# Delta rule: sixteen units in one block on absolute turns, the preparation of a unit begun 44 turns before it

## The chip, the cores and the metric

The program runs on one core of one Trainium2 chip. The metric is the device time of one execution, in microseconds, taken as the median of the runs. The program is a small model of four layers, each with an attention part and a feed-forward part, and everything is computed in float32 (f32). The change lies in one of the eight parts, the attention of the last layer, which takes 1852.8 us of the profiled execution's span (from 2876.4 to 4729.2). A core has an engine for matmuls (PE, its weight loads shown apart as PEld), VectorE (DVE), ScalarE (ACT) and GpSimd (POOL), each with its own instruction stream, and they wait for each other by semaphores. PSUM, where matmuls write, has eight banks here, `P[0]` to `P[7]`.

## The reference, cut to what matters

The last layer's attention is a gated delta rule over 512 tokens, for 8 batches and 8 heads, with keys of 128 and values of 32:

```python
h = layernorm(x) * (1 + ca) + sa
beta = sigmoid(h @ Wb) * 2.0
g = -exp(A_log) * softplus(h @ Wa + dt_bias)
alpha = exp(g)
q = l2norm(silu(causal_conv4(h @ Wq)))      # (8, 512, 8 heads, 128)
k = l2norm(silu(causal_conv4(h @ Wk)))
v = silu(causal_conv4(h @ Wv))              # (8, 512, 8 heads, 32)
def step(state, inp):                       # a scan over the tokens
    q_t, k_t, v_t, a_t, b_t = inp
    retained = einsum('bhvk,bhk->bhv', state, k_t)
    state = a_t * (state - b_t * retained x k_t) + b_t * v_t x k_t
    return (state, einsum('bhvk,bhk->bhv', state, q_t))
out = out * rsqrt(mean(out * out) + 1e-5) * o_norm_w * silu(h @ Wg)
x = x + ga * (out @ Wo)
```

## The kernel before

**Units, chunks, turns.** The work of `delta_rule` is cut into 16 units: a batch and one half (`g`) of its heads, four heads. A unit has four chunks of 128 tokens, and within a chunk the recurrence is solved as a triangular system. A chunk takes nine turns. In each turn every engine is given, in this order: a step that solves the chunk before (table `SOLVE`: state, four solves with a "before" between them, finish), in turns 0, 3 and 6 a part of making the next chunk's matrices (`MAKE`), a step that inverts this chunk's triangular block by products of 32x32 (`INVERT`), and then pieces that prepare the unit that comes next. So a unit has 36 turns, and there is no other order than this one, written out by `in_turn` and followed by all engines alike.

**The pieces.** `norm` is the layer norm (two matmuls of 128x512, once per batch), `small` and `gate` the small vectors of beta and g, `taps` the convolved queries and keys: sixteen pieces of two matmuls of 128x512 each (L1841), every second of which is followed by a silu on ACT (`taps_done`, L1962), a square on POOL (L1918) and a matmul that sums squares (`squares`, L1849). `values`, `keys` (transposes), `norms`, `scale`, `rms` and `out` (the output projection of a batch) are the rest. The matmuls of the chain of chunks are L1778 (state), L1783 and L1790 (before, solve), L1796 and L1803 (finish), L1740 (products of the inversion), L1725 (`MAKE` part 0) and L1733 (parts 1 and 2).

**Blocks.** A `Block` is a piece of program with one stream for each engine, and between two of them is a barrier, `k.end()`, in which the semaphores are cleared. `delta_rule` has ten after its setup: `delta_first` prepares unit 0, `delta_second` runs it, seven of `delta_units` run two units each (first the second half of a batch, with the norm of the next batch among its pieces, then the first half of the next batch, with the output of the batch before), and `delta_last` runs unit 15. In a block a unit's pieces are those of the unit that follows, in turns that `pieces(u)` gives; `taps` stand from turn 1 or 6 to turn 24.

**Banks.** `P[0]` holds the inversion's products, `P[1]` what `MAKE` needs, `P[2]` and `P[7]` take turns as the bank of the solves, `P[3]` (`few`) is for small sums, and `P[4]` to `P[6]` are a ring for the large pieces. A piece of the ring waits (`emptied`) until the one three before it was read. `QK` has queries and keys of 8 heads, so of two units.

**Tables.** ACT works from a table that belongs to a function (silu from one, exp and ln from another); a change is an instruction `ACT_TABLE_LOAD`, either put there by `table` (L1997) or by the compiler before a function that needs it.

## Time and profile before

| what | us |
|---|---|
| median of 3 runs | 4829.73 |
| lowest and highest | 4824.34, 4837.81 |
| the profiled execution, its own time | 4835.91 |
| its span | 4833.6 |
| `delta_first`, from 2876.4 | 64.7 |
| `delta_second`, to 3051.1 | 110.0 |
| the seven `delta_units`, to 4620.6 | 1569.5 |
| `delta_last`, to 4729.2 | 108.6 |

The blocks begin at 2876.4, 2941.0, 3051.1, 3276.0, 3501.2, 3726.8, 3948.2, 4170.7, 4394.8 and 4620.6. A row of the view by stretch gives, for each engine, the busy us in a stretch with the number of instructions, and PEclk, the granted clock of PE as a share of its full speed: 1.00 is 2.4 GHz, 0.50 is 1.2 GHz, and what lies between is a mean of the two over the stretch. In a timeline a row has the start, the length and the instructions, and in brackets the idle time of the engine just before with what ended it. The span in 40 slices shows the stage from slice 24 to 39.

### The profile page before, as it was taken

What the parts mean: (1) busy time and instruction counts of PE and PEld (TensorE: products, weight loads), DVE (VectorE), ACT (ScalarE), POOL (GpSimd) and SP (SyncE); (2) the same over time, 40 slices, a digit from 0 to 9 for tenths busy, and PEclk for the clock granted to TensorE, in tenths of its full rate; (3) what the DMA queues carried; (4) which work ended last, traced back from release to release, by engine and by line L of the source; (5) the groups of instructions that cost most, each with busy time, mean ns of one, the idle gap of its engine ahead of it and who ended that gap; (6) DMA issues with size and microseconds to landing.
All of it is one profiled execution on the core that took longest, in us unless ns stands there. A gap on an engine that the chain in (4) does not pass through costs nothing. (4 is left out here: it accounts for less than half of the span.)

```text
span 4833.6 us, 125108 instructions
## 1 busy us (share of the span) xinstructions
PE 3978.2 (82%) x55640; PEld 2527.1 (52%) x55640; DVE 2423.2 (50%) x6070; ACT 1502.6 (31%) x2781; POOL 746.2 (15%) x740
## 2 busy tenths in 40 slices
PE   3657776999857888888887958999998999999985
PEld 1225664344335565655564324666666666666671
DVE  3556775232277777777771122444343443434344
ACT  2443333455432222222222322323232332323223
POOL 1112221000012212121110002211121212212111
PEclk8777666999855656555556979888898989999966
DMA  2000000322000000000000010000000000000000
GB/s 74 0 0 1 1 1 6 65 35 35 15 1 3 3 3 3 3 3 3 3 3 15 0 54 1 2 2 2 2 2 2 2 2 2 2 2 2 2 2 19
DMA packets 18968, 45.93 MB, mean 10 GB/s; under 512 B 4864, under 2 KB 8320, under 8 KB 17408
## 3 DMA queue, kind: packets, MB, share of 16 engines
q1 hardware_dynamic: 18432, 37.95, 3.2%
q8 instruction: 439, 7.19, 0.6%
q14 instruction: 97, 0.79, 0.1%
HBM read 35.71 MB, written 2.23 MB: 8 GB/s over the span
## 5 line engine op out<-in xcount | busy, mean ns | idle before, releaser
L1841 PE MATMUL ps<-d_hp,d_w_qk 128*128 128x512 f32 x1024 | 519.5, 632 | 8.0 <-ACT d_QK L1962 8.0
L1841 PEld LDWEIGHTS ps<-d_hp,d_w_qk 128*128 128x128 f32 x1024 | 179.0, 193 | 226.1 <-issue 200.8
L1031 PE MATMUL ps<-g_Q,g_K 32*32 32x32 f32 (+1 forms) x12288 | 273.1, 248 | 22.8 <-issue 8.3
L1031 PEld LDWEIGHTS ps<-g_Q,g_K 32*32 32x32 f32 x12288 | 237.9, 135 | 66.7 <-PE ps L1031 38.9
L852 PE MATMUL ps<-ex_hs,w_c_fc 128*128 128x512 f32 x512 | 232.9, 598 | 19.7 <-DVE ex_hs L818 19.7
L1063 PE MATMUL ps<-g_S,g_V 32*64 32x32 f32 x4096 | 160.8, 287 | 86.2 <-DVE g_H L1239 65.0
L1938 ACT ACTIVATE d_F<-ps 128x128 f32<-128x128 f32 x256 | 70.9, 277 | 514.8 <-PE ps L1740 514.3
L863 PE MATMUL ps<-ex_r,w_c_proj 128*128 128x512 f32 x512 | 230.0, 592 | 0.0
L826 DVE TENSOR_TENSOR ex_r<-ex_r 128x512 f32<-128x512 f32 x128 | 88.5, 693 | 277.5 <-ACT ex_r L840 277.5
L840 ACT ACTIVATE ex_r<-ps 128x512 f32<-128x512 f32 x256 | 151.6, 593 | 236.1 <-PE ps L852 236.1
L2070 DVE COPY d_W<-ps 32x128 f32<-32x128 f32 x256 | 73.0, 285 | 278.7 <-PE ps L1790 276.4
L1898 POOL TENSOR_TENSOR d_M<-d_A,w_joins 128x128 f32<-128x128 f32 (+1 forms) x128 | 112.1, 897 | 580.7 <-ACT d_A L1932 580.7
L1063 PEld LDWEIGHTS ps<-g_S,g_V 32*64 32x64 f32 x4096 | 127.7, 203 | 135.3 <-DVE g_H L1239 75.8
L1918 POOL TENSOR_TENSOR d_sq<-d_QK 128x512 f32<-128x512 f32 x128 | 133.3, 1044 | 401.4 <-ACT d_QK L1962 347.9
L2067 DVE TENSOR_TENSOR d_r<-d_r,ps 32x128 f32<-32x128 f32 x192 | 55.0, 286 | 260.6 <-PE ps L1783 244.1
L1047 PE MATMUL ps<-g_V,g_KT 32*32 32x64 f32 x4096 | 156.9, 292 | 21.7 <-issue 1.2
L852 PEld LDWEIGHTS ps<-ex_hs,w_c_fc 128*128 128x128 f32 x512 | 98.3, 192 | 143.8 <-issue 122.9
L1928 ACT ACTIVATE d_D<-d_D 128x512 f32<-128x512 f32 x64 | 40.3, 629 | 412.6 <-DVE d_D L2013 412.6
L863 PEld LDWEIGHTS ps<-ex_r,w_c_proj 128*128 128x128 f32 x512 | 97.3, 190 | 122.5 <-issue 106.7
L1740 PE MATMUL ps<-d_X,d_M 32*32 32x32 f32 x8192 | 128.9, 198 | 38.8 <-DVE d_X L2036 24.3
L1893 POOL TENSOR_TENSOR d_D<-d_D,w_upto 128x512 f32<-128x512 f32 x64 | 85.4, 1335 | 469.7 <-ACT d_D L1928 469.7
L1733 PE MATMUL ps<-d_QK 128*128 128x128 f32 x1024 | 157.2, 300 | 0.8 <-DVE d_P L2018 0.8
(462 smaller groups left out, 8313.4 us busy)
## 6 DMA issues: line engine op xcount, KB each, us to landing
ex_root<-gate_rows SPq DMA_DIRECT2D x8, 2048.0 KB, 15.3
...
```

The lines of the kernel that those rows point to most:

```text
L826: e.tensor_tensor(r[:, n % 2, f], r[:, n % 2, f], r[:, n % 2, f], ALU.mult).then_inc(dve.steps, dve.did(f"r{n}{f}"))
L840: e.activation(r[:, n % 2, f], hidden(f), ACT.Relu).then_inc(act.steps, act.did(f"r{n}{f}"))
L852: e.matmul(hidden(f), k.w["c_fc"][:, n % E, ts(f, C)], hs[:, n % 3], start=True, stop=True).then_inc(pe.steps, pe.did(f"u{n}{f}"))
L863: e.matmul(total(b), k.w["c_proj"][:, x, f, :], r[:, n % 2, f], start=(x == 0 and f == 0), stop=(x == E - 1 and f == F - 1)).then_inc(pe.s ...
L1031: ins = e.matmul(later(scored, n_), keys_, queries(n_, planes, r, 4 * i + j), start=(turn_ == 0 and part == 0 and n_ != 1), stop=(part == ...
L1047: ins = e.matmul(P[2 * odd + 1][ts(h4, 32), 256 + j * 64:320 + j * 64], KT[rows, (KR, KI)[part], i, ts(h4, 32)], V[rows, i, 4 * sg + h4, ( ...
L1063: ins = e.matmul(P[4 + bank][ts(second, 64), t], V[rows, i, 4 * sg + h4, (slice(32, 96), slice(0, 64))[part]], S[rows, i % 2, h4, part, :] ...
L1733: ins = e.matmul(mk[:, ts(h, C)], QK[:, 1, H, t], QK[:, part - 1, H, t], start=True, stop=True)
L1740: ins = e.matmul(inv[rows, h], stationary[rows, h], moving[rows, h], start=True, stop=True, tile_position=(32 * j, 32 * j))
L1841: ins = e.matmul(b, w_qk[:, j, c, ts(H, C)], hp[:, j:j + T], start=(j == 0), stop=(j == TAPS - 1))
L1898: e.tensor_tensor(M[:, a, levels], A32[:, a].unsqueeze(1).to_broadcast([C, many, 4, 32]), k.w["joins"][:, levels].unsqueeze(2).to_broadcas ...
L1918: e.tensor_tensor(squares(x), qk, qk, ALU.mult).then_inc(pool.steps, pool.did(f"{tag}sq{x}"))
```

## The change

All sixteen units stand in one block, and the ten blocks, with the nine barriers between them, are one. A turn has an absolute number, 36 to a unit, and `pieces_at` gives each piece of unit `u` a turn counted from the unit's own start: `norm` 55 turns before (even units), `small` and `gate` from -36 to -27, the sixteen `taps` at -44, -42 and so on to -14, their silu and squares behind them, `values` from -15, `keys` from -10 and `norms` from -9. Within a unit, turns 0 to 22 then hold twelve pieces of `taps` of the next unit and turns 28 to 34 four of the one after, one in every second turn, and turns 23 to 27 hold none. `QK` has 12 heads, three units; `hp`, the normed input with its modulation, has two copies; the norm works in `OT`. One bank, `P[2]`, is for the solves, and the state step now also waits for `out` of the chunk before. The ring has four banks, `P[4]` to `P[7]`, and takes in the norm's first matmul, `small` and the sums of the gates. The norm reads `X`, and the modulation `k.mod`, directly: POOL's copy of a batch (L1905) and DVE's of `modb` (L2098) and `m_out` are gone. The product with `o_norm_w` on POOL stands in a turn of its own (`weigh`). The plain query and key weights are no longer loaded with the layer's other weights, but by a DMA into `QK` in the block `delta_start`, which ends when they are there. A `table` piece stands in every ninth turn. In the delta rule the new program has 195 table loads where there were 127; the matmuls are the same in number and kind.

```diff
-        xb = k.sb("d_xb", [C, T], stack=s)
-        hp = k.sb("d_hp", [C, T + 3], stack=s)
-        QK = k.sb("d_QK", [C, 2, NH, T], stack=s)
+        hp2 = k.sb("d_hp", [C, 2, T + 3], stack=s)
+        hp_of = lambda u: hp2[:, u // 2 % 2]
+        QK = k.sb("d_QK", [C, 2, 12, T], stack=s)
...
+            @block.sync
+            def _(e):
+                e.dma_start(w_plain, k.dram["Wqk3"]).then_inc(dma.steps, dma.did("plain"))
+                e.wait_ge(dma.steps, dma.at("plain"))
...
-        bank = lambda i: P[(2, 7)[i % 2]]
+        bank = lambda i: P[2]
...
+            for turn in range(0, NU * TU, NI):
+                put(0, turn - 1, "table", 0)
+            for u in range(NU):
+                if u % 2 == 0:
+                    for turn, x in ((-55, 1), (-53, 2), (-51, 3)):
+                        put(u, turn, "norm", x)
+                for turn, piece in ((-36, ("small", 0)), (-35, ("gate", 0)), (-33, ("gate", 1)), (-30, ("gate", 2)), (-27, ("gate", 3)), (-27, ("gate", 4))):
+                    put(u, turn, *piece)
...
-                    t = begin + (last - begin) * x // 15
-                    at[t] += [("taps", x)]
-                    if x % 2:
-                        at[12 if 9 <= t + 1 < 12 else t + 1] += [("taps_done", x // 2)]
-                        at[max(t + 3, sums + 2 + x // 2)] += [("squares", x // 2)]
+                    put(u, 2 * x - 44, "taps", x)
+                for x in range(8):
+                    put(u, 4 * x - 41 + (x == 6), "taps_done", x)
+                    put(u, 4 * x - 38, "squares", x)
+                for turn, x in zip((-15, -14, -13, -12), range(NT)):
+                    put(u, turn, "values", x)
+                for turn, x in zip((-13, -12, -11, -11), range(NT)):
+                    put(u, turn, "values_done", x)
+                put(u, -9, "weigh", 0)
+                for x in range(NT - 1):
+                    put(u, 3 * x - 10, "keys", x)
+                    put(u, 3 * x - 9, "keys_done", x)
                 for x in range(5):
...
-                at[3].insert(1, ("table", 0))
-            if u["next"]:
-                for t in (8, 17, 26):
-                    at[t] += [("table", 0)]
+                    put(u, x - 9, "norms", x)
+                put(u, -3, "scale", 0)
+                for turn, x in ((9, 0), (10, 1), (11, 2)):
+                    put(u, TU + turn, "rms", x)
+                if u % 2:
+                    for turn, x in ((13, 0), (14, 1), (16, 2)):
+                        put(u, TU + turn, "out", x)
...
+                for turn in range(min(at), NU * TU + max(max(at) - NU * TU, len(SOLVE)) + 1):
+                    u, i, step = turn // TU, turn % TU // NI, turn % NI
+                    if turn >= 0 and step < len(SOLVE) and 0 < turn // NI <= NU * NT:
+                        n = turn // NI - 1
+                        solve(n // NT, n % NT, *SOLVE[step])
+                    n = turn // NI + 1
+                    if step in MAKE and 0 <= n < NU * NT:
+                        make(n // NT, n % NT, MAKE[step])
+                    if 0 <= turn < NU * TU:
+                        invert(u, i, *INVERT[step])
+                    for piece in at.get(turn, ()):
+                        prepare(*piece)
...
+                if what == "norm" and x < 3 or what in ("small", "values", "keys", "out") or what == "taps" and x % 2 == 0 or (what, x) == ("gate", 2):
+                    ring[u, what, x] = len(order)
+                    order.append((u, what, x))
 
...
+            ring_bank = lambda u, what, x: P[4 + ring[u, what, x] % 4]
...
-                            if c % 2 in outs:
-                                e.wait_ge(dve.steps, dve.at(f"out{outs[c % 2]}"))
-                            outs[c % 2] = n
+                            if u or c:
+                                e.wait_ge(dve.steps, dve.at("out" + (chunk(u, c - 1) if c else chunk(u - 1, 3))))
                             if c:
...
-                            e.matmul(few, k.w["center"][:], xb[:], start=True, stop=True).then_inc(pe.steps, pe.did("nc"))
+                            emptied(e, u, "norm", 1)
+                            e.matmul(ring_bank(u, "norm", 1), k.w["center"][:], flat(k.X[:, u // 2:u // 2 + 1, :]), start=True, stop=True).then_inc(pe.steps, pe.did(tag + "nc"))
...
-        block_of("delta_first", [unit("s", None, None, True, norm=0)])
-        block_of("delta_second", [unit("a", 0, None, True)])
-        for b in range(B - 1):
-            block_of("delta_units", [unit("a", 1, True, True, norm=b + 1), unit("b", 0, True, True, out=b)])
-        block_of("delta_last", [unit("a", 1, True, False, out=B - 1)])
+        all_units("delta_units")
```

**PE, unit 9, turns 7 to 10** (the second half of batch 4). Before, with the sums of the gates (L1858, L1859) and two matmuls of `taps` (L1841) in turn 9:

```order
L1740 MATMUL ps<-d_X,d_M 32x32 x16
L1841 MATMUL ps<-d_hp,d_w_qk 128x512 x2
L1796 MATMUL ps<-d_zz,d_P 128x32 x4
L1740 MATMUL ps<-d_Y,d_F 32x32 x16
L1841 MATMUL ps<-d_hp,d_w_qk 128x512 x2
L1725 MATMUL ps<-w_upto,d_g 128x128 x4
L1858 MATMUL ps<-d_g,w_upto 128x16
L1859 MATMUL ps<-d_g,w_ones 128x16
L1841 MATMUL ps<-d_hp,d_w_qk 128x512 x2
L1790 MATMUL ps<-d_r,d_Y 32x32 x4
```

The same turns now, where L1727 is a solve, L1684 the products, L1733 and L1737 the finish, L1669 `MAKE` part 0, L1771 `taps` and L1779 `squares`:

```order
L1727 MATMUL ps<-d_r,d_Y 32x32 x4
L1684 MATMUL ps<-d_X,d_M 32x32 x16
L1733 MATMUL ps<-d_zz,d_P 128x32 x4
L1684 MATMUL ps<-d_Y,d_F 32x32 x16
L1771 MATMUL ps<-d_hp,d_w_qk 128x512 x2
L1669 MATMUL ps<-w_upto,d_g 128x128 x4
L1727 MATMUL ps<-d_r,d_Y 32x32 x4
L1684 MATMUL ps<-d_X,d_M 32x32 x16
L1771 MATMUL ps<-d_hp,d_w_qk 128x512 x2
```

What stood between `MAKE` part 0 and the solve of turn 10 is gone, and between the `taps` of turn 8 and those of turn 10 there are `MAKE` part 0, a solve and products.

**PE, the end of unit 8 and the start of unit 9.** Before:

```order
L1796 MATMUL ps<-d_zz,d_P 128x32 x4
L1803 MATMUL ps<-d_ze,d_KT 128x32 x4
L1740 MATMUL ps<-d_Y,d_F 32x32 x16
L1710 UNCONDITIONAL_BRANCH
L1711 UNCONDITIONAL_BRANCH
L1778 MATMUL ps<-d_S,d_QK 128x32 x8
L1725 MATMUL ps<-w_upto,d_g 128x128 x4
L1830 MATMUL ps<-d_w_v,d_hp 128x128 x4
L1831 MATMUL ps<-w_Wg,d_hp 128x128
```

Now, where L1715 is the state step and L1754 `small`:

```order
L1733 MATMUL ps<-d_zz,d_P 128x32 x4
L1737 MATMUL ps<-d_ze,d_KT 128x32 x4
L1684 MATMUL ps<-d_Y,d_F 32x32 x16
L1715 MATMUL ps<-d_S,d_QK 128x32 x8
L1669 MATMUL ps<-w_upto,d_g 128x128 x4
L1754 MATMUL ps<-w_Wab,d_hp 128x16 x4
L1771 MATMUL ps<-d_hp,d_w_qk 128x512 x2
```

The two branches of the barrier are gone, the state step and `MAKE` part 0 follow the products at once, and `small` and `taps` stand where `values` stood.

**ACT, the same place.** Before, L1986 being the copy of keys, L1938 that of the products, L1928 the exp of `MAKE`, L1948 the square of the norm and L1958 the silu of values:

```order
L1986 ACTIVATE d_KT<-ps 128x512
L1710 UNCONDITIONAL_BRANCH
L1922 UNCONDITIONAL_BRANCH
L1997 ACT_TABLE_LOAD
L1928 ACTIVATE d_D<-d_D 128x512
L1938 ACTIVATE d_F<-ps 128x128
L1948 ACTIVATE d_sq<-ps 128x512
L1958 ACT_TABLE_LOAD
L1958 ACTIVATE d_values_gates<-ps 128x2x128 x3
```

Now, L1910 and L1864 being the same copies, L1886 the silu of `taps`, L1854 the exp of `MAKE`, L1889 to L1892 the functions of the gates:

```order
L1864 ACTIVATE d_F<-ps 128x128
L1879 ACT_TABLE_LOAD
L1886 ACT_TABLE_LOAD
L1886 ACTIVATE d_QK<-ps 128x512
L1854 ACT_TABLE_LOAD
L1854 ACTIVATE d_D<-d_D 128x512
L1864 ACTIVATE d_F<-ps 128x128
L1889 ACTIVATE d_beta<-d_beta 128x4x4
L1890 ACTIVATE d_t<-d_t 128x4x4
L1892 ACT_TABLE_LOAD
L1892 ACTIVATE d_beta<-d_beta 128x4x4
```

The table of the `table` piece (L1879) is at once followed by another, for the silu of `taps`, and the exp behind it needs a third.

## Rows read from the trace of the kernel before

**Rows 1.** The page, busy time by engine and the granted clock (40 slices of 121 us).

```profile
PE 3978.2 (82%) x55640; PEld 2527.1 (52%) x55640; DVE 2423.2 (50%) x6070; ACT 1502.6 (31%) x2781; POOL 746.2 (15%) x740
...
PEclk8777666999855656555556979888898989999966
```

**Rows 2.** Busy time by stretch: length, busy us of each engine, granted clock, DMA share.

```profile
2876.00:2941.00 65.00, 52.87 (x136) 22.75 (x136) 7.45 (x24) 21.84 (x38) 11.88 (x12) 0.82 0.00 0
2941.00:3051.00 110.00, 97.71 (x1520) 65.03 (x1520) 39.56 (x126) 29.47 (x70) 21.74 (x21) 0.89 0.01 2
...
3501.00:3727.00 226.00, 211.75 (x3217) 144.62 (x3218) 95.39 (x296) 64.85 (x151) 44.20 (x43) 0.89 0.01 2
3727.00:3948.00 221.00, 207.23 (x3216) 140.74 (x3216) 95.19 (x295) 64.46 (x150) 44.19 (x43) 0.92 0.01 2
...
4621.00:4729.00 108.00, 87.95 (x1560) 76.89 (x1559) 47.72 (x144) 22.46 (x49) 10.99 (x10) 0.61 0.01 2
```

**Rows 3.** The same view, two stretches inside the pair that begins at 3726.8.

```profile
3755.00:3784.00 29.00, 28.86 (x397) 15.47 (x395) 14.54 (x44) 12.78 (x28) 8.30 (x8) 1.00 0.01 2
...
3926.00:3947.00 21.00, 19.71 (x380) 16.43 (x380) 10.72 (x36) 4.60 (x15) 2.94 (x3) 0.74 0.01 2
```

**Rows 4.** The same view around two falls of the clock.

```profile
3809.00:3812.50 3.50, 3.42 (x58) 3.34 (x59) 1.15 (x6) 1.42 (x2) 1.04 (x1) 0.98 0.00 0
3812.50:3819.00 6.50, 6.50 (x41) 4.57 (x44) 2.62 (x10) 0.63 (x1) 0.35 (x1) 0.50 0.01 4
...
3863.50:3867.00 3.50, 2.01 (x50) 1.76 (x49) 2.33 (x7) 0.70 (x2) 0.54 (x1) 0.99 0.00 0
3867.00:3870.40 3.40, 3.40 (x5) 0.87 (x4) 2.21 (x7) 0.97 (x6) 1.11 (x1) 0.50 0.00 0
```

**Rows 5.** Timeline of PE in unit 8: start, length, instructions, idle before and its releaser.

```profile
3858.57 1.98 PE L1841 MATMUL ps<-d_hp,d_w_qk 128*128 128x512 f32 x4 [1.00 <-ACT d_QK L1962]
...
3863.50 1.05 PE L1725 MATMUL ps<-w_upto,d_g 128*128 128x128 f32 x8
...
3866.41 0.45 PE L1740 MATMUL ps<-d_X,d_M 32*32 32x32 f32 x32 [1.49 <-DVE d_X L2036]
3866.79 3.66 PE L1841 MATMUL ps<-d_hp,d_w_qk 128*128 128x512 f32 x4
...
3872.09 1.98 PE L1841 MATMUL ps<-d_hp,d_w_qk 128*128 128x512 f32 x4
...
3879.41 1.02 PE L1849 MATMUL ps<-d_sq,w_picks 128*8 128x512 f32 x2 [1.58 <-POOL d_sq L1918]
```

**Rows 6.** Timeline of PE in unit 9, the same turn of its unit.

```profile
3978.80 1.96 PE L1841 MATMUL ps<-d_hp,d_w_qk 128*128 128x512 f32 x4
...
3980.97 0.45 PE L1740 MATMUL ps<-d_X,d_M 32*32 32x32 f32 x32
```

**Rows 7.** Timeline at the end of the block that ends at 3948.

```profile
3946.17 0.29 DVE L2087 TENSOR_TENSOR d_S<-d_S,ps 128x128 f32<-128x128 f32 x1 [2.32 <-PE ps L1803]
...
3946.69 0.29 DVE L2090 TENSOR_TENSOR d_O<-d_o,d_qn 128x128 f32<-128x128 f32 x1
...
3948.23 1.46 PE L1778 MATMUL ps<-d_S,d_QK 128*128 128x32 f32 x6 [1.51 <-PEq L70]
```

**Rows 8.** Timeline of PE at a finish step of unit 8, turn 26.

```profile
3920.98 1.41 PE L1796 MATMUL ps<-d_zz,d_P 128*128 128x32 f32 x8 [2.27 <-DVE d_ze L2076]
```

**Rows 9.** Groups of ACT by line: busy us and mean ns, idle before them.

```profile
L1955 ACT ACT_TABLE_LOAD x56 | 71.8, 1283 | 1.0
L1962 ACT ACT_TABLE_LOAD x40 | 51.3, 1283 | 0.7
```

**Rows 10.** Timeline of ACT, a table load and the function after it.

```profile
2895.30 1.28 ACT L1962 ACT_TABLE_LOAD   x1
2896.60 0.60 ACT L1962 ACTIVATE d_QK<-ps 128x512 f32<-128x512 f32 x1
```

**Rows 11.** DMA issues, KB each, median us from issue to landing.

```profile
w_Wqk<-in_Wqk_dram SPq DMA_DIRECT2D x1, 1024.0 KB, 4.6
```

366 lines of the change are left out of this document (123 added, 243 removed).

## The prediction, as written before the changed kernel ran

> **What bounds the kernel now.** I read the page's busy line and clock line first [rows 1], then busy time by stretch [rows 2, 3], then the places where PE's clock falls [rows 4], then PE's timeline with its idle times [rows 5 to 8]. PE is the busiest engine (82% of the span, DVE 50%, ACT 31%) [rows 1]. In the delta rule this is sharper: in a block of two units PE is busy 207.2 of 221 us, DVE 95, ACT 64, POOL 44 [rows 2]. PE sets the time, so only three things can move it: matmul work, PE's waits, and its clock. The change leaves the work as it is. The clock is the large lever. A pair takes 226 us at a granted 0.89 and 221 at 0.92 [rows 2] with the same instructions; with two levels, 1.2 and 2.4 GHz, 0.92 means 2 x 0.08 x 221 = 35 us at the low one, 0.89 means 50 us (48 with the mean of 0.90 over the pairs). A stretch full of `taps` is granted 1.00 with PE busy 28.86 of 29; the last chunk, without `taps`, 0.74 [rows 3].
>
> **What a us at the low clock costs.** Four matmuls of `taps` took 3.66 us low and 1.98 high [rows 5], so a low us loses 0.46 us where PE is full. Across pairs, 0.03 of clock on 226 us is 13.4 us low for 5 us of time, 0.37. I use 0.40 to compare pairs. At full clock the pair of 221 us would take 221 - 0.40 x 35 = 207.
>
> **What makes the clock fall.** Twice: with PE busy 2.01 of 3.5 us it went to 0.50 for the next 3.4 us; and, more telling, with PE busy 3.42 of 3.50 us, but on small products, it was 0.50 for the next 6.5 us [rows 4]. Being busy is not enough here; stretches without 512-wide matmuls fall. The Trainium skill ("TensorE: Matmul & The Clock Gate", Part 1: The HAM clock gate) says that the clock follows how busy PE has been lately. Read as busy time, the 3.42 of 3.50 contradicts it, and by it a pair with its waits gone would hardly fall; that is the first rival below.
>
> **The change part by part, for a pair (two units), at full clock, from 207.**
> - *Barrier.* PE idles 1.51 us for it, and DVE and ACT start behind [rows 7]; 1.0 more for that, estimated. -2.5.
> - *Ring of four, taps evenly in every second turn.* In unit 8 `taps` waited 1.00 us for a bank that ACT had yet to read, and `squares` 1.58 us for POOL [rows 5]. With four banks and silus four turns apart both go: -2.6 in this unit. The other unit of the pair I take at half of that (bounds 0 and 2.6): -4 together.
> - *One solve bank.* The state step now waits for `out` of the chunk before, not only for S: DVE finished S at 3946.17 + 0.29 and `out` at 3946.69 + 0.29, so 0.5 us later [rows 7]. PE stands idle for it only where no `taps` lie behind the products: turn 35 of both units and turn 17 of one. Behind it in PE's stream is everything, `MAKE` part 0 too. 3 x 0.5 = +1.4; were all eight exposed, +4.
> - *Places that lose their cover.* With two `taps` matmuls between `MAKE` part 0 and the solve, products of turn 10 had no idle time in unit 9 [rows 6]; without, 1.49 us in unit 8 [rows 5]. Now unit 9 has none either: +1.5, and 0.5 for turn 27, where no `taps` stand. The finish step's 2.27 us in turn 26 [rows 8] stays, since turns 23 to 27 are as bare as before. +2.
> - Together 207 - 2.5 - 4 + 1.4 + 2 = 204.
>
> **The clock after.** `taps` were packed (two turns of three) and left chunk 3 bare; now one turn in two has them, and turns 28 to 34 too. So chunk 3, at 0.74 before, fills up, while dense chunks get thinner. I count the stretches without `taps` between two pieces of them: 9 to 10, 17 to 18 (odd units), 23 to 27, and 35 to 0 in each unit, eight or so in a pair, of which I expect four of five to drop the clock, for 3.4 to 6.5 us each as in [rows 4]: about 30 us low in a pair (bounds 8 and 60). At 0.40 to 0.46 each that is +12.5, so a pair takes 216.5 against a mean of 224.3 (1569.5 / 7). I round to 216: **-8.3 a pair, -58 in seven**.
>
> **The ends.** *First pieces of the next unit.* By starting 44 turns ahead, four pieces of `taps`, a norm, a square and small sums leave the seven pairs and go into the start. `taps` are 8 x 0.49 = 4.0 us [rows 5]; the rest I estimate at 3.7 from the same 0.49 for a wide matmul (two of the norm, two of squares, and small ones). -7.7 here. *Start.* First and second block take 64.7 + 110.0 us with PE busy 52.9 and 97.7 [rows 2]. The moved 7.7 us fall into the wait at the first block's end (some 12 us of its 65 are idle), a barrier goes (-2.5), the bare end of unit 0 fills: 174.7 to 170, -4.7. *End.* The last block runs at 0.61 [rows 2]; its chain of DVE and PE stays, a barrier goes, out waits come: -1.6.
> *Setup.* The load of the plain weights took 4.6 us to landing [rows 11], hidden among the layer's other loads; now little of DVE's setup runs beside it. +4 (bounds 0 and 5). The copies of `X` and `modb`, which go, cost nothing on PE's path, save at the very start of the stage, where PE waits for the first, which I leave in the rounding.
>
> **Table loads.** 68 more at 1283 ns [rows 9] are 87 us of ACT, 5.5 us a unit: ACT goes from 64.5 to about 75.5 of 216 us. The function after a load began 1.30 us after the load's start [rows 10], so nothing beyond the load is lost. The Trainium skill ("ScalarE: Activation LUTs", What ACT_TABLE_LOAD costs) adds a drain of 1380 ns to each; by that the 68 would be 181 us of ACT, still not the bound; these rows show no drain. On PE's path a load counts where PE waits for a function behind it: the exp of `MAKE` once a unit, which has three turns until PE needs it, and copies of products, which PE waits for. I take 0; if the exp's load came through in every unit, 16 x 1.28 = +21 us, and that is in the range.
>
> **Sum.** -58 - 7.7 - 4.7 - 1.6 + 4 = -68. The profiled execution took 4835.91 (span 4833.6), 6.2 over the median of 4829.73. So 4768 for a run like the profiled one, 4762 for the median; I say **4765 us**.
>
> **Rivals.**
> 1. *The clock hardly falls.* If a piece of `taps` in every second turn is enough to hold it, some 8 us a pair are low: 204 + 3.5 = 207.5, -16.8 x 7 = -118, with the ends -128: **4702**. For it: 29 us at 1.00 where PE was full [rows 3]. The rule of the Trainium skill named above, with PE busy some 97% of the time, leads here too. Against it: the fall after 3.42 of 3.50 busy [rows 4]. Chance 0.23.
> 2. *Little gain.* The removed waits return behind others (the ze wait behind the out wait, table loads before the copies), or 40 us stay low: a pair 220 to 223, in all **4800 to 4815**. Chance 0.12.
> 3. *No change.* The same with some 45 us low, a pair 224, and start, end and setup adding up to little: within 14.5 us of **4830**. Chance 0.11.
> 4. *Slower: thinner `taps` keep the clock down.* Place: the dense chunks 0 to 2, which today run at up to 1.00 [rows 3]. Before, the clock that had fallen was back at 1.00 after four wide matmuls in a row [rows 4, 5]; with one piece of two matmuls every second turn it may stay low through whole chunks. Price 0.46 us for each low us. From 204, it decides at (224.3 - 204) / 0.46 = 44 us low a pair; at 60 low a pair takes 204 + 27.6 = 231.6, +51 in seven pairs, less 10 at the ends: **about 4870**. Against it: chunk 3 at 0.74 with no `taps` at all [rows 3] is as thin as it can be and is only 21 us long. Chance 0.14.
> That the change does not do what it says is no rival of its own: the order of instructions shows the barriers gone and the matmuls equal.
>
> **Numbers.** Forecast, 4735 to 4800: 0.40. The five cases make 1.00. The range, **4695 to 4840**, takes in the forecast, rival 1 down to 4695, rivals 2 and 3 and the table loads' +21; outside are the slower case and the tail of rival 1. A measurement of this kernel can tell about 0.3%, 14.5 us, from no change. Faster by more: 0.40 + 0.23 + 0.12 = 0.75. Within: 0.11. Slower by more: 0.14. The likeliest case's own range is 4735 to 4800.
>
> **What the new profile would show.** Right: one stretch from about 2880 to 4660 with no idle PE released by PEq of L70; pairs of 72 turns of 216 us at a mean clock of 0.93; no wait of `taps` for ACT; DVE, ACT and POOL at 95, 75 and 44 us a pair. ACT at 75 with PE's waits for copies of products unchanged would bear out that the tables cost nothing. Wrong: a mean clock under 0.89 (rival 4), or over 0.97 (rival 1); more idle time before the products released by ACT's copies (the tables do cost); the state step idle for more than 0.5 us, released by DVE's `out` (the single bank costs more than 1.4 a pair).

## The result, and the profile after

The changed kernel is slower. The medians of 20 runs each are 4887.4 us after (4834.8 to 4906.2) and 4838.2 before (4824.3 to 4851.5); the ratio, by means, is 1.0093, 95% interval 1.0075 to 1.0111: +49 us by the medians and +45 by the ratio, where -65 had been forecast. The profiled execution of the new kernel took 4903.9 us (span 4902.1), 16.6 over its median; that of before is 2.3 under its own.

The page after, to be laid beside [rows 1]: busy time by engine, and the granted clock in 40 slices.

```profile
PE 4039.4 (82%) x55640; PEld 2534.4 (52%) x55640; DVE 2419.0 (49%) x6054; ACT 1586.7 (32%) x2849; POOL 741.6 (15%) x732
...
PEclk8776666999855665556557979898988898888866
```

The matmuls are the same in number (55640), and PE is busy 61 us longer for them. ACT is busy 84 us longer: 68 table loads of 1.283 us are 87. The view by stretch, for one pair of units (two units, 72 turns) of the new kernel (length, PE busy, PEld, DVE, ACT and POOL, then the granted clock):

```profile
3290.60:3526.00 235.40, 220.75 (x3217) 146.14 (x3217) 94.73 (x293) 75.74 (x159) 43.53 (x42) 0.86 0.01 2
```

The same view of the kernel before, for a pair cut at the same turns:

```profile
3363.80:3588.80 225.00, 211.33 (x3217) 143.24 (x3218) 95.29 (x295) 64.66 (x150) 44.20 (x43) 0.89 0.01 2
```

A pair went from 225.0 (its like in [rows 2]) to 235.4 us. PE idles 14.7 us in it for 13.7, and is busy 220.8 for 211.3: the time went into the same matmuls at a lower clock. A granted 0.86 is 2 x 0.14 x 235.4 = 66 us at 1.2 GHz, 0.89 is 49.5. With a clock of two digits such a figure is good to some 2 us; the stretches at 0.50, added up one by one in the traces, give 64.7 for this pair of the new kernel, and on the mean of the seven pairs 64.5 after (pair 234.2 us, idle 15.0) and 44.8 before (224.2, idle 13.8). PE's groups by line in the seven pairs of the new kernel (busy us and mean ns, then the idle time before the group and its releasers):

```profile
L1771 PE MATMUL ps<-d_hp,d_w_qk 128*128 128x512 f32 x880 | 498.7, 694 | 0.0
...
L1715 PE MATMUL ps<-d_S,d_QK 128*128 128x32 f32 x673 | 118.3, 341 | 13.0 <-DVE d_O L2012 11.4 <-DVE d_O L2006 1.6
L1684 PE MATMUL ps<-d_X,d_M 32*32 32x32 f32 x7168 | 109.1, 195 | 51.9 <-DVE d_X L1959 39.9 <-DVE d_X L1962 12.1
```

The same groups of the kernel before:

```profile
L1841 PE MATMUL ps<-d_hp,d_w_qk 128*128 128x512 f32 x896 | 453.6, 629 | 7.0 <-ACT d_QK L1962 7.0
...
L1849 PE MATMUL ps<-d_sq,w_picks 128*8 128x512 f32 x224 | 126.4, 649 | 11.0 <-POOL d_sq L1918 11.0
L1778 PE MATMUL ps<-d_S,d_QK 128*128 128x32 f32 x673 | 119.3, 343 | 11.1 <-PEq L70 10.9
L1740 PE MATMUL ps<-d_X,d_M 32*32 32x32 f32 x7168 | 111.6, 197 | 31.0 <-DVE d_X L2036 20.4 <-DVE d_X L2039 10.1
```

A matmul of `taps` took 694 ns on average for 629. The waits went as the edits would have it: `taps` for ACT (7.0 us in seven pairs) and `squares` for POOL (11.0), of which [rows 5] showed one each, are gone, the barrier's 10.9 [rows 7] too; the state step waits 13.0 for DVE's `out`, and the products 51.9 for 31.0.

By stage: setup +2.2 us (the first block begins at 2878.6 for 2876.4), start and unit 0 -1.9, the seven pairs +69.9, unit 15 -4.0.

Where the clock falls in the new kernel, by stretch, in turns 21 to 31 of unit 5 (the turns 23 to 27, bare of `taps`, lie on both sides of the change from the first row to the second):

```profile
3589.00:3604.30 15.30, 13.51 (x258) 10.33 (x256) 5.93 (x13) 4.93 (x13) 2.76 (x3) 1.00 0.01 3
3604.30:3624.80 20.50, 19.21 (x169) 14.29 (x169) 4.97 (x19) 1.39 (x3) 2.48 (x2) 0.50 0.00 1
```

PE's timeline of the same place (start, length, instructions, idle time before and its releaser):

```profile
3603.70 1.41 PE L1733 MATMUL ps<-d_zz,d_P 128*128 128x32 f32 x8 [1.79 <-DVE d_ze L1998]
...
3610.05 3.46 PE L1715 MATMUL ps<-d_S,d_QK 128*128 128x32 f32 x16
...
3617.23 0.65 PE L1684 MATMUL ps<-d_X,d_M 32*32 32x32 f32 x32 [1.29 <-DVE d_X L1959]
...
3619.60 3.78 PE L1771 MATMUL ps<-d_hp,d_w_qk 128*128 128x512 f32 x4
```

A finish step that waited 1.79 us for DVE, then state, `MAKE` part 0 and products that waited 1.29, without a piece of `taps`, stand at the start of 20.5 us at 1.2 GHz, in which PE is busy 19.2. PE had been busy 13.5 of the 15.3 us before (as in [rows 4], where it was busy 3.42 of 3.50 us before a fall). Those 20.5 us are the longest of eight low stretches of a pair; the others last 3.4 to 10.2 us. All eight begin at one of three places, each after a wait: at the products of turn 1 of a chunk, which wait for DVE's x0 (turn 10 of both units, 28 of one), at the finish step (turn 26 of both), and at the state step right behind a finish (turn 18 of one unit, turn 35 to 0 twice).

The kernel before had such stretches too. In its seven pairs there are 42, 7.5 us long on average, and 17 of them last 10.2 us; the new kernel has 55, of 8.2 us. The one of before that follows the finish step of [rows 8]:

```profile
3921.60:3931.80 10.20, 10.20 (x75) 8.92 (x74) 3.02 (x13) 0.00 (x0) 0.00 (x0) 0.50 0.00 0
```

### The profile page after: what moved, and what is told of

Its sections match the earlier page's. It is cut to its first block and busy times, and to the rows that moved or that the text cites. A ratio compares the mean times of both kernels' runs of the same rounds, so it can differ in the third digit from the quotient of the medians.

```text
span 4902.1 us, 125016 instructions
## 1 busy us (share of the span) xinstructions
PE 4039.4 (82%) x55640; PEld 2534.4 (52%) x55640; DVE 2419.0 (49%) x6054; ACT 1586.7 (32%) x2849; POOL 741.6 (15%) x732
## 5 line engine op out<-in xcount | busy, mean ns | idle before, releaser
L1771 PE MATMUL ps<-d_hp,d_w_qk 128*128 128x512 f32 x1024 | 573.7, 689 | 2.7 <-DVE d_hp L2023 2.7
L1771 PEld LDWEIGHTS ps<-d_hp,d_w_qk 128*128 128x128 f32 x1024 | 193.8, 209 | 164.6 <-issue 149.6
L852 PE MATMUL ps<-ex_hs,w_c_fc 128*128 128x512 f32 x512 | 232.6, 598 | 19.2 <-DVE ex_hs L818 19.2
L1864 ACT ACTIVATE d_F<-ps 128x128 f32<-128x128 f32 x256 | 70.5, 275 | 518.6 <-PE ps L1684 517.7
L840 ACT ACTIVATE ex_r<-ps 128x512 f32<-128x512 f32 x256 | 151.6, 593 | 235.4 <-PE ps L852 235.3
L1684 PE MATMUL ps<-d_X,d_M 32*32 32x32 f32 x8192 | 126.1, 197 | 60.6 <-DVE d_X L1959 45.3
L1854 ACT ACTIVATE d_D<-d_D 128x512 f32<-128x512 f32 x64 | 40.3, 629 | 418.1 <-DVE d_D L1937 418.0
L597 PE MATMUL ps<-att_kg,att_qx 32*128 32x96 f32 x1024 | 121.7, 354 | 41.5 <-DVE att_qx L511 27.0
```

Source lines behind the costliest of these rows:

```text
L597: ins = e.matmul(scored[:, g, b], qx[ts(g, 32), q, 4 * u + b, :, :].rearrange("p h q -> p (h q)"), kg[ts(g, 32), q, 4 * u + b, :], start=T ...
L840: e.activation(r[:, n % 2, f], hidden(f), ACT.Relu).then_inc(act.steps, act.did(f"r{n}{f}"))
L852: e.matmul(hidden(f), k.w["c_fc"][:, n % E, ts(f, C)], hs[:, n % 3], start=True, stop=True).then_inc(pe.steps, pe.did(f"u{n}{f}"))
L1684: ins = e.matmul(inv[rows, h], stationary[rows, h], moving[rows, h], start=True, stop=True, tile_position=(32 * j, 32 * j))
L1771: ins = e.matmul(b, w_qk[:, j, c, ts(H, C)], hp_of(u)[:, j:j + T], start=(j == 0), stop=(j == TAPS - 1))
```

## The experiments

Seventeen kernels ran beside the kernel before. All but the ones named otherwise differ from the changed kernel only in `pieces_at`, the table of turns. For each, one pair of its profiled execution and the mean of its seven are given in the table at the end of this section. **Low** is the time at 1.2 GHz: 2 x (1 - clock) x length. Ratios are against the kernel before, run beside each group of experiments (4836.9 to 4840.3 us).

### First question: the clock, or the waits?

**e1_dense.** `taps` packed as before, same start:

```diff
-                    put(u, 2 * x - 44, "taps", x)
...
+                    t = 23 * x // 15 - 44
+                    put(u, t, "taps", x)
+                    if x % 2:
+                        put(u, t + 1, "taps_done", x // 2)
+                        put(u, t + 3, "squares", x // 2)
```

(silu and squares follow one and three turns behind, in this and all kernels that move `taps`, unless told. In the changed kernel the squares are four turns behind, so these kernels move them too, and e11_squares shows that this alone can matter.)

> The changed kernel with the taps of a unit packed as before, in two turns of three (from -44 to -21) instead of every second turn to -14; their silu one turn and their squares three turns behind; nothing else differs. Theory A (thinner taps keep PE's clock down): while the taps last the clock stays at 2.4 GHz for whole chunks, and is low in the bare turns behind them; a pair of units goes from 235.6 us with 65 us at the low clock to 222-228 with 40-50, the program to 4790-4850. Theory B (the new waits cost: the single solve bank, table loads, the uncovered turns): those are all still there, so the pair stays at 233-238 and the program at 4870-4900.

Measured: 4982.2 us, 1.0304 (1.0279 to 1.0329). Both were missed: dense `taps` are slower by another 95 us, with low time as high as in the changed kernel (66 us a pair on the mean) and idle time up from 15.0 to 21.6. Packing also makes the stretch without `taps` longer, twelve turns (16 to 27) for five, and 10.2 and 13.7 us at the low clock begin in it, at the finish and the state step.

**e2_even.** `taps` over all 36 turns:

```diff
-                    put(u, 2 * x - 44, "taps", x)
...
+                    t = 9 * x // 4 - 47
+                    put(u, t, "taps", x)
```

> The changed kernel with the sixteen taps of a unit spread evenly over all 36 turns (one in every 2.25 turns, from -47 to -14), so that turns 23 to 27 are no longer bare; silu and squares behind them. Theory A1 (the bare turns 23 to 27 start the long low stretch that the thin taps then can't end): low time falls from 65 to 40-50 us a pair, pair 226-230, program 4810-4840. Theory A2 (thin taps as such keep the clock down, wherever they stand): low time grows or stays, 65-90 us a pair, pair 235-246, program 4880-4960. Theory B (waits): no change beyond 5 us a pair.

Measured: 4681.1 us, 0.9681 (0.9656 to 0.9706), the fastest kernel of the study, 157 us under before and 206 under the changed one. One pair of it, by stretch:

```profile
3335.80:3537.20 201.40, 193.00 (x3218) 129.37 (x3217) 94.15 (x293) 77.02 (x160) 45.34 (x42) 0.97 0.01 2
```

The clock is 0.97 and the idle time 8.4 us. A2 and B fall; A1 had the sign, and well under half of the size (47 to 77 us for 206).

**e3_fill.** Useless work in the bare turns. These matmuls are not part of the computation and nothing reads them:

```diff
+                for x, turn in enumerate((23, 25, 27)):
+                    put(u, turn, "fill", x)
...
+                        if what == "fill":
+                            emptied(e, u, "fill", x)
+                            for n in range(2):
+                                e.matmul(ring_bank(u, "fill", x), k.w["ident"][:], w_v[:].rearrange("p j f -> p (j f)")[:, 0:512], start=True, stop=True)
```

> The changed kernel with useless work added: two more 128x512 matmuls in each of the turns 23, 25 and 27 of every unit, whose result nobody reads, into a bank of the ring. That is 6 x 0.49 = 2.9 us of PE a unit at full clock, 5.9 us a pair, 47 us in the program. Theory A (the clock): the long low stretch from turn 23 on (20 us in odd units) breaks up, low time falls from 65 to 35-45 us a pair (-20 to -30, worth -8 to -13 us), so that the pair gets no longer or shorter in spite of more work: 228-236 us, program 4830-4890. Theory B (waits, not the clock): the work adds up or hides in idle time, low time stays near 65; pair 237-241, program 4900-4930.

Measured: 4804.2 us, 0.9929 (0.9908 to 0.9949): 83 us less than the changed kernel, more than A had it, and with twice the work that was expected. A matmul of the program is two instructions on PE, so the two matmuls of a turn are four of 0.49 us:

```profile
3450.95 1.98 PE L1749 MATMUL ps<-d_w_v,w_ident 128*128 128x512 f32 x4
```

The expectations of this and the other kernels with useless work count one instruction for each matmul. By the traces the work is 11.7 us a pair and 94 in the program, not 5.9 and 47. In all seven pairs the low stretches that began in turns 26 and 28 are gone; those in turns 10, 18 and 0 are left.

**e9_fill_elsewhere.** Its control, the same work between pieces of `taps`:

```diff
+                for x, turn in enumerate((5, 13, 21)):
+                    put(u, turn, "fill", x)
```

> The control for the useless work in turns 23, 25 and 27: the same six matmuls a unit, in turns 5, 13 and 21, where taps stand in the turns on either side. Theory A (the bare turns 23 to 27 are what lets the clock fall for long): low time stays at 55-65 us a pair, the work adds up, pair 236-242, program 4890-4930. Rival (any more wide work holds the clock): as with the fill in 23, 25 and 27, low 20-30 us, pair 220-225, program 4800-4830.

Measured: 4959.8 us, 1.0253 (1.0229 to 1.0278), 72 us over the changed kernel and above both expectations. Low time fell here too, to 51 us a pair on the mean for 64.5, so the control isn't clean: the fills take banks of the ring, and `values` and `out` then wait for ACT (some 3 us a pair). But the same work costs 156 us less in the bare turns. Not all of that is the clock: between the two kernels idle time differs by 8.7 us a pair, 61 in seven, since the work in turns 23 to 27 also stands where PE waited for DVE. Low time differs by 27 us a pair, at the price found below (0.46) 12.4, 87 in seven. That settles the first question: mostly the clock, and with it what stands in turns 23 to 27.

**e8_before_fill.** The kernel before with the same useless work in turns 25, 28, 31 and 34 of each unit, written as in e3_fill:

```diff
+                for x, t in enumerate((25, 28, 31, 34)):
+                    at[t] += [("fill", x)]
```

> The kernel before with useless work added: two more 128x512 matmuls in turns 25, 28, 31 and 34 of every unit, its bare end, into a bank of the ring; 8 us a pair at full clock. Theory A: the low stretches at the units' ends (12 us in chunk 3 of each unit, and what follows) break up, from 47 us low a pair to 10-25; -22 to -37 us low are worth -9 to -15 us, and +8 of work, part of it in idle time: pair 215-223, program 4770-4825. Rival (the clock is low there for another reason than missing wide matmuls): pair 230-233, program 4880-4900.

Measured: 4857.6 us, 1.0037 (1.0019 to 1.0055). Low time fell from 45 to 26 us a pair on the mean (15 to 37), near what was expected, but the time lies between the two expectations: of 127 us of added work (256 instructions; 63 had been expected) 21 show. The kernel before was paying for the same thing, but its fill is no gain.

### Second question: tables and banks

**e5_tables.** One silu ahead of the table piece:

```diff
-                    put(u, 4 * x - 41 + (x == 6), "taps_done", x)
+                    put(u, 4 * x - 41 + (x == 6) - (x == 1), "taps_done", x)
```

> The changed kernel with one silu (taps_done 1) a turn earlier, at -38 in place of -37, so that it stands ahead of the table piece of turn 35 and not behind it: 60 table loads fewer in the program (174 for 234; before had 166). Theory T (the added table loads delay what PE waits for): a load stands ahead of the exp and the copies at each unit's start; the pair gets 2-5 us shorter, program 4850-4870. Theory A (the clock alone): ACT is 9.6 us a pair less busy and PE's waits and the pair stay within 1 us, but for what another phase of the clock does; program 4875-4900.

Measured: 4848.6 us, 1.0023 (1.0008 to 1.0038), 39 us less and just under T's range. Two of its seven pairs, by stretch:

```profile
3359.60:3581.40 221.80, 208.00 (x3218) 138.40 (x3217) 93.83 (x293) 65.46 (x151) 43.51 (x42) 0.92 0.01 2
4027.40:4260.00 232.60, 218.99 (x3218) 147.35 (x3218) 93.95 (x293) 65.46 (x151) 43.49 (x42) 0.86 0.01 2
```

The same instructions take 221.8 us at 0.92 and 232.6 at 0.86, with equal idle time. So most of the gain is the clock, which in more than half of the pairs fell into another pattern; against the changed kernel at an equal 0.86 it is 2.8 us a pair. These two rows also give a price of a low us: 10.8 us for 29.6 by the rounded clock, 0.37. Added up one by one, the low stretches are 37.5 and 63.6 us, so it is 0.41; over the first six pairs of this kernel, and as well of e4_two_banks and e12_even_two_banks, it is 0.45 to 0.47.

**e6_even_tables.** The same idea on e2_even (174 loads for 238):

```diff
-                    for turn, x in ((-55, 1), (-53, 2), (-51, 3)):
+                    for turn, x in ((-56, 1), (-54, 2), (-52, 3)):
...
-                        put(u, t + 1, "taps_done", x // 2)
-                        put(u, t + 3, "squares", x // 2)
+                        put(u, t + 1 + 3 * (x == 1), "taps_done", x // 2)
+                        put(u, t + 3 + 3 * (x == 1), "squares", x // 2)
```

> The changed kernel with taps spread evenly over 36 turns (as in e2_even), and the silu of the first run three turns later, next to the second's, and the norm one turn earlier: 174 table loads in the program for 238 in e2_even. Theory T (loads delay PE somewhat, as the 2.5 us a pair at an equal clock that e5_tables gave): pair 197-201 for 201.4, program 4650-4680. Theory A alone: pair 201 +- 1 if the clock stays at 10 us low, program 4675-4690.

Measured: 4685.7 us, 0.9683 (0.9659 to 0.9706), no difference from e2_even; a pair is 201.5 us for 201.4 (two of the seven took 204 to 205, with 17 us low), with ACT busy 65 for 77. With the clock steady, 64 table loads cost nothing that can be measured.

**e4_two_banks** and **e12_even_two_banks**. Two banks for the solves and three in the ring, and the waits that belong to them, on the changed kernel and on e2_even:

```diff
-        bank = lambda i: P[2]
+        bank = lambda i: P[(2, 7)[i % 2]]
...
-            ring_bank = lambda u, what, x: P[4 + ring[u, what, x] % 4]
+            ring_bank = lambda u, what, x: P[4 + ring[u, what, x] % 3]
...
-                n = ring[u, what, x] - 4
+                n = ring[u, what, x] - 3
```

> The changed kernel with the banks as before: P[2] and P[7] take turns for the solves, the ring has three banks, and the state step waits for out of the chunk two before. Theory A (the clock is nearly all of it): the waits of the state step for d_O (13.3 us in 6.7 pairs, 2 us a pair) go; the pair is 232-237 us with 60-65 us low, program 4870-4900. Theory W (the single bank is a main cost): pair under 228, program under 4850.

> e2_even with the banks as before: two for the solves, three in the ring. At the high clock the cost of the banks can be read without the clock's noise. Theory: the state step's waits for d_O (9.2 + 5.1 us in seven pairs, 2 us a pair) go and waits of ring pieces for ACT come (43 us in six pairs in e4_two_banks, 7 us a pair): pair 203-209, program 4690-4740. Rival: the single bank is the dearer, pair 198-201, program 4655-4680.

Measured: 4881.7 us, 1.0093 (1.0057 to 1.0129), the changed kernel's time; and 4707.1 us, 0.9728 (0.9692 to 0.9764), 26 us over e2_even. In the first, idle time rises from 15.0 to 20.2 us a pair on the mean of seven and low time falls from 64.5 to 42; A had the program's time, neither theory the low time. In the second, at 0.97 on either side, the pair shown takes 204.1 for 201.4, all of it idle time, and the mean of seven is 205.2 for 202.0, with 2 us of low time in it, as the theory had it. The change's use of the banks is right, by some 3 us a pair.

### Third question: how long the bare stretch, or where?

**e10_two_gaps.** Two bare stretches of three turns for one of five:

```diff
-                    put(u, 2 * x - 44, "taps", x)
...
+                    t = 2 * x - 44 + 2 * (x >= 8) - 2 * (x < 0)
+                    put(u, t, "taps", x)
```

> The changed kernel with the five bare turns (23 to 27) split in two stretches of three: the second half of the taps is two turns later, so that turns 7 to 9 and 25 to 27 are bare. Spacing of the others stays at every second turn. Theory A (the length of a bare stretch decides, not how thin the taps are): low time lies between the 65 us a pair of five bare turns and the 10 us of none over two, 20-45; pair 208-222, program 4730-4810. Rival (only the number of bare turns counts, 5 or 6 here as there): low 60-70, pair 233-238, program 4870-4910.

Measured: 4760.1 us, 0.9832 (0.9796 to 0.9869); low 39 us. As A had it, with the squares a turn nearer to their `taps` as well.

**e15_one_fill.** Useless work in turn 25 alone, which nothing reads:

```diff
+                for x, turn in enumerate((25,)):
+                    put(u, turn, "fill", x)
```

> The changed kernel with useless work in turn 25 alone (two 128x512 matmuls), so that the five bare turns are two and two: 2 us of work a pair. Theory A: low falls from 65 us a pair nearly as far as with three fills (24): 20-35, pair 217-224, program 4775-4820. Rival (the low stretches come from the units' borders and the 9th and 17th turns as well, one fill does little): low over 45, pair over 228, program over 4850.

Measured: 4818.8 us, 0.9956 (0.9942 to 0.9970), with 20 to 41 us low and 32 us of added work, twice what was expected: A, at its edge. The falls in turn 26 are gone, that in turn 28 is not.

**e14_gap_moved.** All `taps` five turns earlier, and silu and squares with them:

```diff
-                    put(u, 2 * x - 44, "taps", x)
+                    put(u, 2 * x - 49, "taps", x)
...
```

> The changed kernel with all taps, silus and squares five turns earlier (-49 to -19): the five bare turns stand at 18 to 22 of a unit for 23 to 27, taps in odd turns. Table loads 251 for 234. Theory A (a bare stretch of five turns costs it wherever it is): low 50-75 us a pair, pair 230-242, program 4850-4940. Rival (it was the place): low under 35, pair under 222, program under 4810.

Measured: 4857.5 us, 1.0032 (1.0019 to 1.0046); 41 us low in five pairs of six. The time is A's, low time and pair (225 us) lie between the two: the same gap elsewhere costs less, but costs.

**e13_even_later.** e2_even one turn later, `taps` in turns 8, 1, 3, 5 of a chunk for 7, 0, 2, 4:

```diff
-                    t = 9 * x // 4 - 47
+                    t = 9 * x // 4 - 46
```

> e2_even with all taps, silus and squares one turn later (-46 to -13), so that taps stand in turns 8, 1, 3 and 5 of every chunk for 7, 0, 2 and 4: no stretch of more than two bare turns, at other places of the chunk. Theory A (no long bare stretch, wherever the taps stand): low time 5-25 us a pair, pair 199-210, program 4670-4735. Rival (the places within the chunk made it: taps ahead of the finish step and behind the state step): low over 35, pair over 212, program over 4745.

Measured: 5048.5 us, 1.0423 (1.0397 to 1.0449), the slowest of all, 367 us over e2_even. There is no bare stretch over two turns in it. A is out and the rival came true, so length is not the whole cause. PE's groups by line in six of its pairs:

```profile
L1685 PE MATMUL ps<-d_X,d_M 32*32 32x32 f32 x6144 | 96.9, 197 | 69.3 <-DVE d_X L1960 60.4 <-DVE d_X L1963 8.9
...
L1734 PE MATMUL ps<-d_zz,d_P 128*128 128x32 f32 x384 | 65.8, 322 | 50.3 <-DVE d_ze L1999 44.8 <-DVE d_zz L1996 5.5
L1761 PE MATMUL ps<-d_w_v,d_hp 128*128 128x128 f32 x384 | 57.3, 296 | 28.6 <-ACT d_QK L1887 28.6
```

The first two of these groups in seven pairs of e2_even:

```profile
L1685 PE MATMUL ps<-d_X,d_M 32*32 32x32 f32 x7231 | 112.2, 196 | 16.2 <-DVE d_X L1963 10.8 <-DVE d_X L1960 5.2
...
L1734 PE MATMUL ps<-d_zz,d_P 128*128 128x32 f32 x448 | 57.1, 272 | 5.6 <-DVE d_ze L1999 5.0 <-DVE d_zz L1996 0.5
```

The products wait 69.3 us for DVE's x0 for 16.2, the finish step 50.3 for 5.6. `taps` in turn 0 stand ahead of the first, `taps` in turn 7 ahead of the second; moved one turn on, they stand behind. The low stretches begin there too: of the twelve that begin between 3600 and 3845 us, five begin at a finish step, five at the products of turn 1, and two where `values` waited 2.4 us for ACT. A pair, by stretch, idles 27.6 us and has 59 us low; five of the seven took 252 to 254 us, with 75 to 79 low:

```profile
3438.90:3684.90 246.00, 218.40 (x3219) 141.68 (x3218) 96.05 (x293) 73.49 (x157) 43.33 (x42) 0.88 0.01 2
```

**e16_bunched.** Turns 7, 8, 0 and 1 of each chunk, so that both places are covered and five turns of every chunk are bare:

```diff
-                    t = 9 * x // 4 - 47
+                    t = 9 * (x // 4) - 47 + (0, 1, 2, 3)[x % 4]
```

> As e2_even four pieces of taps a chunk, but in turns 7, 8, 0 and 1 for 7, 0, 2 and 4: they cover the finish step and the turn in which PE waits for DVE's x0, and leave five bare turns (2 to 6) in every chunk, with squares in turns 2 and 4. Table loads rise to 325. Theory P (what counts is that the two long waits of a chunk have taps in front of them): low under 30 us a pair, pair under 212, program under 4745. Theory L (a bare stretch of five turns brings the clock down wherever it is): low over 50 us, pair over 222, program over 4800.

Measured: 4779.7 us, 0.9876 (0.9860 to 0.9893). A pair of it by stretch:

```profile
3567.20:3782.20 215.00, 198.07 (x3218) 133.05 (x3217) 94.34 (x293) 92.20 (x172) 43.68 (x42) 0.95 0.01 2
```

A group of PE by line, in six pairs:

```profile
L1685 PE MATMUL ps<-d_F,d_Y 32*32 32x32 f32 x4480 | 67.7, 201 | 48.2 <-ACT d_F L1865 47.8
```

The clock is 0.95, with five turns without `taps` in each chunk: for the clock P, and not L. But two of these turns hold a `squares`, 512 wide too, so that no more than two in a row are without a wide matmul; L is out for `taps`, not for wide matmuls of any kind. The time is longer than P allowed since PE now waits 48 us in six pairs for ACT's copies, which stand behind table loads (325 of them in the program, ACT busy 92 us a pair). Here, other than in e6_even_tables, the loads do cost.

**e17_even_b.** The third and the fourth piece of each chunk a turn later than in e2_even. The expectation speaks of turns 7, 0, 2 and 5, with one piece moved; the kernel as written has them in 7, 0, 3 and 5:

```diff
-                    t = 9 * x // 4 - 47
+                    t = 9 * (x // 4) - 47 + (0, 2, 5, 7)[x % 4]
```

> e2_even with the fourth piece of taps of each chunk in turn 5 for 4 (turns 7, 0, 2, 5, twice three turns apart at 5 and 7). Table loads 238 as in e2_even. Theory P (turns 7 and 0 covered is what counts): low 5-20 us a pair, pair 199-206, program 4665-4705. Rival (the even spacing counts): low 20-40, pair 206-215, program 4710-4760.

Measured: 4837.0 us, 0.9994 (0.9980 to 1.0007), with 24 to 31 us low in six pairs and 18.9 idle. Neither: the low time is the rival's (20 to 40; P had 5 to 20), though turns 7 and 0 are covered, and the time is over both, since `squares` now wait for POOL (33 us in six pairs) and `values` for ACT (29). Two of four pieces moved by one turn, and with them their silus and squares, cost 156 us.

**e11_squares.** e2_even with both `squares` of a chunk in turn 1, ahead of the 1.86 us in which the step of turn 2 waits for d_W:

```diff
-                        put(u, t + 3, "squares", x // 2)
+                        put(u, t + (10 if x % 4 == 1 else 6), "squares", x // 2)
...
-                    put(u, x - 9, "norms", x)
+                    put(u, x - 8, "norms", x)
```

> e2_even with the squares matmuls moved to the second turn of a chunk, two together, ahead of the step that waited 1.86 us for DVE's d_W there (norms a turn later). Theory: at a clock of 0.97 a pair now takes 201.4 us of which 193 are PE busy; the idle time before the solve steps falls by 2-4 us a pair, pair 197-200, program 4650-4675, if the clock stays. Rival: the two squares side by side take wide matmuls from other turns, low time goes from 10 to 20-30 us, and the pair gets no shorter (200-208).

Measured: 4735.5 us (4719.5 to 4757.4, and the profiled execution is the slowest), 0.9774 (0.9727 to 0.9822), 54 over e2_even. The rival had the direction and too small a size: idle time fell by 2.3 us a pair, but low time rose from 10 to 44. All its falls in a pair begin at a finish step or just behind it, at the state step and `MAKE` part 0; in e2_even a `squares` stood in turn 7, right ahead of the finish, and here none does. That this is the reason was not tested.

**e7_even_tail.** e6_even_tables with useless work, read by nothing, from 11 turns ahead of unit 15 to the end:

```diff
+            for x, turn in enumerate(range(-11, 44, 2)):
+                put(NU - 1, turn, "fill", 10 + x)
```

> e6_even_tables with useless work at the end of the stage only: two 128x512 matmuls in every second turn from turn -11 of unit 15 to its turn 43, 28 pairs, 27 us of PE at full clock, where no taps are left and the clock was 0.6 (54 to 60 us low in the last seven chunks of 170 us). Theory A: most of the work fits in idle time and the clock comes back: low 5-20 us there, the tail 8-20 us shorter, program 4665-4678 against 4686. Rival (the tail hangs on the chain of DVE and PE latency and not on the clock): the added work lengthens it, program 4690-4710.

Measured: 4714.1 us, 0.9727 (0.9689 to 0.9764), 28 over e6_even_tables. In the profiled execution the last seven chunks take 188 us for 170, at 0.89 for 0.82. The added work is 112 instructions, 55 us at full clock and 67 as it ran, where 27 had been expected; it costs more than the clock gives back. How much of the tail hangs on the clock this run can't tell: its profiled execution (4754.0) is 40 us over its median, and four of its pairs ahead of the added work already had 24 to 31 us low where e6_even_tables had 10 to 17.

### One pair of each, from the view by stretch

| kernel | median | pair | PE busy | idle | clock | low | mean of 7 | its low |
|---|---|---|---|---|---|---|---|---|
| before | 4838.2 | 225.0 | 211.3 | 13.7 | 0.89 | 50 | 224.2 | 44.8 |
| changed | 4887.4 | 235.4 | 220.8 | 14.7 | 0.86 | 66 | 234.2 | 64.5 |
| e1_dense | 4982.2 | 241.4 | 218.2 | 23.2 | 0.88 | 58 | 241.2 | 66 |
| e2_even | 4681.1 | 201.4 | 193.0 | 8.4 | 0.97 | 12 | 202.0 | 14 |
| e3_fill | 4804.2 | 221.3 | 212.6 | 8.7 | 0.95 | 22 | 220.3 | 24 |
| e9_fill_elsewhere | 4959.8 | 239.3 | 221.8 | 17.5 | 0.91 | 43 | 241.0 | 51 |
| e8_before_fill | 4857.6 | 228.6 | 217.0 | 11.6 | 0.94 | 27 | 227.8 | 26 |
| e5_tables | 4848.6 | 221.8 | 208.0 | 13.8 | 0.92 | 36 | 224.2 | 45 |
| e4_two_banks | 4881.7 | 228.4 | 208.2 | 20.2 | 0.92 | 37 | 229.1 | 42 |
| e12_even_two_banks | 4707.1 | 204.1 | 192.9 | 11.2 | 0.97 | 12 | 205.2 | 16 |
| e6_even_tables | 4685.7 | 201.5 | 193.6 | 7.9 | 0.97 | 12 | 202.9 | 16 |
| e10_two_gaps | 4760.1 | 215.2 | 208.2 | 7.0 | 0.91 | 39 | 215.5 | 42 |
| e15_one_fill | 4818.8 | 219.2 | 207.9 | 11.3 | 0.94 | 26 | 221.5 | 35 |
| e14_gap_moved | 4857.5 | 225.3 | 209.4 | 15.9 | 0.91 | 41 | 226.2 | 48 |
| e13_even_later | 5048.5 | 246.0 | 218.4 | 27.6 | 0.88 | 59 | 250.3 | 75 |
| e16_bunched | 4779.7 | 215.0 | 198.1 | 16.9 | 0.95 | 22 | 215.2 | 25 |
| e17_even_b | 4837.0 | 224.2 | 205.3 | 18.9 | 0.93 | 31 | 221.8 | 29 |
| e11_squares | 4735.5 | 215.0 | 208.9 | 6.1 | 0.90 | 43 | 215.1 | 47 |
| e7_even_tail | 4714.1 | 211.7 | 203.7 | 8.0 | 0.93 | 30 | 209.6 | 27 |

The last two columns are the mean of the seven pairs between the first turn of unit 1 and that of unit 15, with the stretches at 0.50 added up one by one. The seventh pair holds no `taps` of a next unit in its last turns and has more low time than the others in most kernels. One pair can mislead: that of e13_even_later is among its shortest. What a kernel's total has besides lies mostly ahead of the pairs: they begin at 3055 us in the changed kernel, at 3081 in e1_dense and 3095 in e13_even_later.

Over the first six pairs of the fourteen kernels without added work, PE is busy 188.7 us plus 0.49 for each low us, within 2 us in all 84. With the added work taken off, the four kernels with fills inside the pairs fit as well. So a pair is that work, plus idle time, plus nearly half of the low time. Between before and the changed kernel, on the means, idle time gives 1.2 us and 19.7 more low us at 0.46 give 9.1, of 10.0.

## Why the prediction was wrong

**The bound.** Right: PE sets the time, and its clock is the lever. The kernels are told apart by idle time and clock.

**The term that failed is the low time after**, "about 30 us low in a pair". It was 64.5 on the mean of the seven. The places were right: the seven that the prediction names all had a fall, and turn 28 of one unit was the eighth. What it had wrong is how many of them drop the clock, four in five for all of them, and above all for how long: it took 3.4 to 6.5 us for each, from the two falls of [rows 4], and the eight last 8.1 us on average in the pair shown, with one of 20.5 and two of 10.2. The trace of before had the sign: its 42 low stretches last 7.5 us on average, and eight of those would have been 60. 34.5 us more than forecast at 0.46 are 16 us a pair and 111 in seven, nearly the whole gap from 4765 to 4887. The bounds of the term, 8 and 60, did not hold it either, and since it alone decided the sign, a chance of 0.14 for slower was too small.

**The break-even was right**: it was put at 44 us low, at 0.46 each; 64.5 gives 204 + 0.46 x 64.5 = 233.7, measured 234.2. **Rival 4 came true in its time (4870 for 4887) and not in its reason.** It blamed thin `taps`. Thinner ones, at 2.25 turns, gave 0.97, and dense ones gave a slower kernel with as much low time. What the runs put in its place: the clock falls where PE waits and has only small products around the wait, at the finish step with the state step behind it and at turn 1 of a chunk. It fell far less with `taps` right ahead of both (e2_even and e16_bunched against e13_even_later), and it stayed low longest where no `taps` stand for turns on end (turns 23 to 27: e3_fill, e10_two_gaps, e15_one_fill). In the changed kernel turn 7 is bare in two chunks of four and turn 0 in the other two; turn 8 is bare ahead of the three falls at a state step.

**The pair at full clock**, forecast 204, comes out at 234.2 - 0.46 x 64.5 = 204.5, and that is luck, for two errors cancel. The start was too high: before, 224.2 - 0.46 x 44.8 = 203.6, not 207. And the waits together did not save 3 us but cost about 1: the barrier brought 1.6 us (10.9 / 7) for 2.5; `taps` and `squares` brought 2.6 (18.0 / 7) for 4, so the other unit of the pair had next to nothing of the kind; the single bank cost 1.9 for 1.4, in waits of up to 0.85 us; the places without cover cost 3.0 (51.9 - 31.0 over 7) for 2. Each was small and on the dear side. That the single bank was no mistake stands by e12_even_two_banks.

**Rival 1, the clock hardly falls**, was not what this change did. Its price, 4702 for a kernel with 8 us low, was not far off: e2_even has 10 low and took 4681, but PE also idles 6 us a pair less in it than in the changed kernel. The rule of the Trainium skill ("TensorE: Matmul & The Clock Gate", Part 1: The HAM clock gate) is that the clock follows how busy PE has been. If busy is read as PE's busy time, these traces don't agree: the changed kernel's pair was busy 94% of the time at 0.86, e16_bunched's 92% at 0.95.

**The ends.** Start and unit 0 -1.9 for -4.7, the last unit -4.0 for -1.6, setup +2.2 for +4: right in sign, and together -3.7 for -2.3. The -7.7 of work moved out of the pairs can't be read apart, but its first term was too small: a piece of `taps` is four instructions and 1.98 us in [rows 5], so four pieces are 7.9 us and not 4.0; the seven pairs have 880 instructions of `taps` for 896.

**Table loads.** 84 us more of ACT, as forecast (87), and no drain on either side of a load: in e16_bunched ACT ran a function from 3500.00 for 0.22 us, a load from 3500.23, and the next function from 3501.53. That they cost nothing was right for e6_even_tables. In the changed kernel they cost at most 2.8 us a pair (e5_tables at an equal clock), within the +21 kept for the range.

**What stays open**: which activity of the array in which order makes the clock fall or hold. Two `squares` moved (e11_squares) took it from 0.97 to 0.90 with less idle time, e17_even_b covers both places and had 27 us low a pair over six pairs, where e2_even had 10, and e14_gap_moved lies between the theories. The cover of the two places explains the large steps, not these. Nor do single pairs repeat: pairs of e5_tables with the same instructions had 37 and 54 us low.
